# Depthwise convolution, two group norms and a per-row rotation in fp32: beginning, statistics order, transition and second-half loads redone, rotation begun at step 19

## The reference

```python
x = x + conv5x5_depthwise(groupnorm(x), K)          # x: 16 images, 128 channels, 64x64, fp32
x = x + einsum('hvc,bchw->bvhw', R, groupnorm(x))   # R: one 128x128 matrix for each image row h
# groupnorm: 32 groups of 4 channels, mean and variance over (4, 64, 64) of one image, eps 1e-5, no weights
# K: 8 of the 9 weights of a channel, each used once as +w (POS_IDX) and once as -w (NEG_IDX), 9 of 25 places zero
```

## Time and profile before

| | |
|---|---|
| runs of the kernel, without profile | 471.43 us (470.09, 471.43, 472.82) |
| profiled execution, its own time | 474.42 us |
| its span, first to last instruction | 472.5 us |
| last matmul ends / last output store lands | about 442 us / the end of the span |
| TensorE busy | 405.8 us (86%), granted clock 0.963 on the mean |
| VectorE, ScalarE, GpSimd busy | 361.3, 265.8, 232.0 us |
| DMA | 140.63 MB, 298 GB/s over the span |

### The profile page before, as it was taken

How to read it: one execution, slowest core, us unless ns; L and a number is a source line. 1 busy time by engine, 2 the same in 40 slices (tenths; PEclk the granted TensorE clock), 3 DMA queues, 4 the chain that set the end, 5 groups by cost and what they waited for, 6 DMA issues and landing times.

```text
span 472.5 us, 8427 instructions
## 1 busy us (share of the span) xinstructions
PE 405.8 (86%) x3104; PEld 195.0 (41%) x3104; DVE 361.3 (76%) x701; ACT 265.8 (56%) x516; POOL 232.0 (49%) x297
## 2 busy tenths in 40 slices
PE   0498979999999999999999999999995799999400
PEld 0154434555555555554444444434441334444100
DVE  2669999999999999998777877766665678888300
ACT  1144647576766756777666555566633377777000
POOL 3544666676756756776456544454211244545000
PEclk9999999999999999999999999999997999999855
DMA  8805558889998678997598999999979999999995
GB/s 306 365 1 171 188 179 240 281 304 365 372 297 273 207 255 314 388 361 272 185 313 304 324 313 337 312 305 304 307 233 300 308 207 420 379 389 418 427 428 250
DMA packets 33512, 140.63 MB, mean 298 GB/s; under 512 B 3392, under 2 KB 3648, under 8 KB 20800
## 3 DMA queue, kind: packets, MB, share of 16 engines
q1 hardware_dynamic: 16000, 106.24, 63.5%
q10 hardware_dynamic: 17472, 33.85, 20.6%
HBM read 72.96 MB, written 67.12 MB: 296 GB/s over the span
## 4 chain that ended last, share of the span: by engine, by line
PE 71%; DVE 16%; ACT 2%; issue 2%; DMA 2%; ACTq 1%; DVEq 0%
PE ps L612 47%; PE ps L645 23%; DVE stats L514 4%; DVE area L503 2%; DVE area L500 2%; DVE stats L522 2%; DMA rot<-in_taps_first_dram 2%; ACT gn L447 2%; DVE tin L552 1%; DVE dev L542 1%; DVE affine L530 1%; ACT std L459 1%; PE ps L622 1%; DVE affine L532 1%; ACTq L439 1%
## 5 line engine op out<-in xcount | busy, mean ns | idle before, releaser
L612 PE MATMUL ps<-area 64*64 64x496 f32 (+2 forms) x2560 | 287.0, 591 | 7.8 <-issue 4.4
L612 PEld LDWEIGHTS ps<-area 64*64 64x64 f32 x2560 | 137.0, 134 | 107.1 <-issue 97.2
L364 POOL TENSOR_TENSOR area<-mask,area 128x325 f32<-128x325 f32 x128 | 131.9, 1055 | 71.6 <-PE ps L612 53.8
L645 PE MATMUL ps<-gn,rot 128*128 128x512 f32 x256 | 118.6, 608 | 11.6 <-DVE tin L552 7.6
L464 ACT ACTIVATE area<-area,affine 128x256 f32<-128x256 f32 x190 | 96.9, 588 | 30.4 <-DVE affine L532 30.4
L430 ACT ACTIVATE area<-ps 64x512 f32<-64x512 f32 x128 | 75.8, 592 | 42.7 <-PE ps L612 40.1
L522 DVE BATCH_NORM_STATS2 stats<-area 128x6 f32<-128x512 f32 x128 | 80.8, 692 | 0.8
L514 DVE BATCH_NORM_STATS2 stats<-area 128x6 f32<-128x512 f32 x128 | 80.3, 690 | 0.0
L645 PEld LDWEIGHTS ps<-gn,rot 128*128 128x128 f32 x256 | 46.7, 192 | 79.5 <-issue 66.6
L379 POOL TENSOR_SCALAR area<-area,affine 128x256 f32<-128x256 f32 x62 | 46.9, 766 | 65.8 <-DVE affine L532 65.8
L459 ACT ACTIVATE std<-ps,eps 128x16 f32<-128x16 f32 (+1 forms) x36 | 9.8, 273 | 76.7 <-PE ps L622 76.7
(11 more groups left out here) (19 smaller groups left out, 74.9 us busy)
## 6 DMA issues: line engine op xcount, KB each, us to landing
area<-in_x_dram SPq DMA_DIRECT2D x31, 1024.0 KB, 7.3
x_scratch<-area ACTq DMA_DIRECT2D x62, 512.0 KB, 9.6
out_dram<-tin SPq DMA_DIRECT2D x16, 1024.0 KB, 10.2
out_dram<-area SPq DMA_DIRECT2D x16, 1024.0 KB, 25.4
tin<-x_scratch SPq DMA_DIRECT2D x13, 1024.0 KB, 12.5
area<-x_scratch SPq DMA_DIRECT2D x13, 1024.0 KB, 12.3
rot<-in_rota_dram SPq DMA_DIRECT2D x4, 1024.0 KB, 10.8
tin<-x_scratch SPq DMA_DIRECT2D x3, 896.0 KB, 17.5
```

The lines of the kernel that those rows point to most:

```text
L364: last = nc.gpsimd.tensor_tensor(taps[k % TRING][:, c * KW:(c + 1) * KW].rearrange("p d (b r) -> p d b r", r=TAPS), bass.AP(tensor=of_rows ...
L612: last = nc.tensor.matmul(ps[half, bank + c].rearrange("p (j w) -> p j w", j=J)[:, :, outs], taps[k % TRING][rows, (2 * pair + c) * KW + d ...
L645: nc.tensor.matmul(ps[:, rot_bank(m), :], rot[:, n % UNITS * RH + h], gn[n % NRING][:, h], start=True, stop=True).then_inc(rotated, 1)
```

## The change

The beginning: taps come once, unsigned (two DMAs, not four), and the signs are in the mask, which now has one 65-wide band for each of the 5 offsets and is made by GpSimd with 4 more affine_selects, a memset and 10 small tensor_scalars; GpSimd starts on taps only after the first spread is formed; VectorE normalises 3 images of step 0, ScalarE 5; x is measured at most 2 steps ahead in place of 3, the first steps written out. The statistics: VectorE's order in a step changes, own and other adds become two functions, the sums of steps 30 and 31 share the last round (ROUNDS = 35), the averages of mean and spread share bank 7. The rotation: it begins at step 19 and ends there with 13 granules kept (KEPT) before the convolution ends; its four matmuls follow each other at the end of a step, over banks 4, 5, 6, later seven banks. The transition: the last averages stand between rotations of granule 13; norm2 of the last steps of each half goes by small DMAs on SyncE's queue. The loads: six granules of the second half are loaded early from step 28 on, each with the channels that are stored by then (80, 88, 96, 104, 112, 112), the gap up to channel 111 after send_norms of step 29, the last 16 channels after the last x1 store; the other loads and the stores are written out. Host side, the taps arrays are laid out without the plus and minus parts.

```diff
-ROUNDS = STEPS_ALL + LAG
-FILL = 4
+ROUNDS = STEPS_ALL + LAG - 1
+FILL = 2
 POOL_J = 2
-DVE_J = 4
+DVE_J = 3
 RH = 4
 UNITS = H // RH
 GRANULES = 2 * UNITS
-START = 21
+START = 19
 KEPT = STEPS_ALL - START
 DRING = 5
 NRING = 2
+ROT_BANKS = 3
 POOL_IMAGES = 3
 ROT_LOADS = 4
 ROT_STEP = 8
-EARLY_STEPS = PER_HALF - 2
-EARLY = EARLY_STEPS * 2 * GC
-EARLY_COUNT = 6
-NORM2_BATCH = PER_HALF - 2
+NORM2_BATCH = (PER_HALF - 2, PER_HALF - 4)
+EARLY_STEP = 28
+EARLY = tuple(range(EARLY_STEP, EARLY_STEP + 5)) + (EARLY_STEP + 4,)
 def conv_rotate_kernel(nc, x, taps_first, taps_rest, rota, out):
...
-        SWITCH = 2 * (START - 1)
+        SWITCH = 2 * START
         def bank_of(q):
-            return 2 * (q % 3) if q < SWITCH else 2 * ((q + 1) % 2)
+            return 2 * (q % 3) if q < SWITCH else 2 * (q % 2)
...
+        LAST_THREE = KEPT * RH - 1
         def rot_bank(m):
-            return 4 + m % 2 if m < (KEPT + 1) * RH else m % 6
...
+            e = n - UNITS
+            if not 0 <= e < len(EARLY):
+                return 16
+            return 48 if channels_before(EARLY[e] - 2) < LATE else 32
...
+            r, half, first = sum_round(k), k // PER_HALF, k % PER_HALF * 2 * GC
+            queue.wait_ge(affine_ready, r + 1)
+            for n in range(2):
+                queue.dma_start(norm2[first + n * GC:first + (n + 1) * GC, half].rearrange("c k j -> c (k j)"),
+                                affine[n * HALF:n * HALF + GC, r, sum_place(k)].rearrange("p k j -> p (k j)")
+                                ).then_inc(norm2_sent, 16)
         def load_granule(queue, n, channels):
             u = n % UNITS
...
+            sp.dma_start(row_rest.rearrange("p r d -> p (r d)"), taps_rest).then_inc(taps_landed[1], 16)
+            for k in range(4, XRING):
+                load_x(k)
+            for s in range(2, STEPS_ALL + 1):
+                sp.wait_ge(x1_ready, 2 * (s - 1))
...
                     sp.dma_start(rot[:, rows], rota[:, rows]).then_inc(rot_landed, 16)
+                if s == PER_HALF + 1:
...
                     load_granule(sp, 1, slice(0, C))
...
...
+                if s == STEPS_ALL - 1:
+                    store_norms(1)
+                if s == STEPS_ALL:
+                    load_norms(1)
+                    send_norms(sp, STEPS_ALL - 4)
+                n = s - START + 2
+                if n >= 2:
+                    if n >= DRING:
+                        sp.wait_ge(out_stored[n - DRING], 16)
+                    load_granule(sp, n, slice(0, C))
+                for e in range(len(EARLY)):
+                    if EARLY[e] == s:
+                        await_stores(sp, s - 3)
+                        if e == 5:
+                            sp.wait_ge(stats_ready, measured(s - 3 + LAG))
+                        load_granule(sp, UNITS + e, slice(0, channels_before(s - 2)))
+            send_norms(sp, STEPS_ALL - 3)
+            for e in range(len(EARLY)):
+                if channels_before(EARLY[e] - 2) < LATE:
+                    load_granule(sp, UNITS + e, slice(channels_before(EARLY[e] - 2), LATE))
+            send_norms(sp, STEPS_ALL - 2)
+            send_norms(sp, STEPS_ALL - 1)
+            await_stores(sp, STEPS_ALL - 1)
+            for e in range(len(EARLY)):
+                load_granule(sp, UNITS + e, slice(LATE, C))
             store_granule(sp, KEPT - 1)
...
             sp.wait_ge(convolved, 2 * STEPS_ALL)
+            load_granule(sp, 22, slice(0, C))
...
+            for rows in (slice(0, 2), slice(2, RH)):
+                store_rows(sp, GRANULES - 1, rows)
...
+            for n, (d, sign) in enumerate(((0, 1.0), (1, -1.0), (3, -1.0), (4, 1.0))):
+                pool.wait_ge(middle_ready, n + 1)
+                nc.gpsimd.affine_select(out=near_middle[:], in_=near_middle[:], compare_op=ALU.not_equal, fill=sign,
+                                        base=d - PAD, pattern=[[-1, HALF + BAND]], channel_multiplier=1
+                                        ).then_inc(middle_ready, 1)
...
+            for n in range(2):
+                half, window = slice(n * HALF, (n + 1) * HALF), slice(n * HALF, n * HALF + BAND)
+                for d, source, sign in ((0, near, 1.0), (1, near, -1.0), (2, near_middle, 1.0), (3, near, -1.0),
+                                        (4, near, 1.0)):
+                    nc.gpsimd.tensor_scalar(mask[half, d], source[half, window], sign, None, ALU.mult
+                                            ).then_inc(mask_ready, 1)
...
+            pool.wait_ge(spread_ready, 1)
+            spread_taps(0, (0, 1))
+            spread_taps(0, (2, 3))
+            pool.wait_ge(spread_ready, 2)
+            spread_taps(1, (0, 1))
+            normalise(1)
+            spread_taps(1, (2, 3))
+            pool.wait_ge(spread_ready, 3)
+            spread_taps(2, (0, 1))
+            normalise(2)
+            spread_taps(2, (2, 3))
+            spread_taps(3, (0, 1))
+            spread_taps(3, (2, 3))
+            for s in range(FILL, STEPS_ALL - 1):
                 if group(s + 2):
...
+            act.dma_start(row_first.rearrange("p r d -> p (r d)"), taps_first).then_inc(taps_landed[0], 16)
...
+            s = STEPS_ALL - 1
+            evict(s - 1, 1)
+            take_root(s + 1)
+            normalise_rows(KEPT)
+            evict(s, 0)
+            store(act, s - 1)
+            take_root(s + 2)
+            evict(s, 1)
+            store(act, s)
+            normalise_rows(KEPT + 1)
+            take_root(s + 3)
+            for n in range(KEPT + 2, GRANULES):
...
                 c, bank = 2 * pair, bank_of(2 * k + pair)
...
+            def add_other(k, pair):
+                c = 2 * pair + 1
                 dve.wait_ge(y_ready, 2 * (2 * k + pair + 1))
...
+            measure(0, (0, 2, 1, 3))
+            deviate(0)
+            scale(0)
+            dve.wait_ge(affine_ready, 1)
+            for j in range(DVE_J):
+                last = nc.vector.tensor_scalar(normed[0][:, :, j], xin[0][:, j], affine[:, 0, 0, 0, j:j + 1],
+                                               affine[:, 0, 0, 1, j:j + 1], ALU.mult, ALU.add)
+            last.then_inc(normed_dve, 1)
+            measure(1)
+            measure(2, (0,))
+            deviate(1)
+            measure(2, (1, 2, 3))
+            scale(1)
+            add_own(0, 0)
+            measure(3, (0, 1))
+            deviate(2)
+            measure(3, (2, 3))
+            add_other(0, 0)
+            scale(2)
+            add_own(0, 1)
+            add_other(0, 1)
+            measure_sum(0)
+            deviate(3)
+            add_own(1, 0)
+            add_other(1, 0)
+            for s in range(FILL, START):
+                measure(s + 2)
+                scale(s + 1)
+                add_own(s - 1, 1)
+                add_other(s - 1, 1)
+                measure_sum(s - 1)
+                deviate(s + 2)
+                add_own(s, 0)
+                add_other(s, 0)
+            for s in range(START, STEPS_ALL - 1):
+                add_own(s - 1, 1)
+                if group(s + 2):
+                    measure(s + 2)
+                scale(s + 1)
+                add_other(s - 1, 1)
+                measure_sum(s - 1)
+                deviate(s + 2)
+                add_own(s, 0)
+                add_other(s, 0)
+                add_rows(s - START, range(RH))
+            s = STEPS_ALL - 1
+            add_own(s - 1, 1)
+            scale(s + 1)
+            add_other(s - 1, 1)
+            measure_sum(s - 1)
+            deviate(s + 2)
+            add_own(s, 0)
+            add_other(s, 0)
+            add_own(s, 1)
+            scale(s + 2)
+            add_other(s, 1)
+            measure_sum(s)
+            add_rows(KEPT - 1, (0, 1))
+            deviate(s + 3)
+            add_rows(KEPT - 1, (2,))
+            scale(s + 3)
+            add_rows(KEPT - 1, (3,))
+            for n in range(KEPT, GRANULES):
                 add_rows(n, range(RH))
...
+            for half in (low, high):
+                average_mean(0, half)
+            for half in (low, high):
+                average_spread(0, half)
+            for at, d in enumerate(OFFSETS):
+                convolve(0, 0, d)
+                if at in (2, 3):
+                    average_mean(1, low if at == 2 else high)
+                if at == 4:
+                    average_spread(1, low)
+            for at, d in enumerate(OFFSETS):
+                convolve(0, 1, d)
+                if at == 0:
+                    average_spread(1, high)
+                if at in (2, 3):
+                    average_mean(2, low if at == 2 else high)
+            for s in range(1, STEPS_ALL):
                 for at, d in enumerate(OFFSETS):
+                    convolve(s, 0, d)
+                    if at in (0, 1):
+                        average_spread(s + 1, low if at == 0 else high)
                 for at, d in enumerate(OFFSETS):
+                    convolve(s, 1, d)
+                    if at in (0, 1):
```

(42 more changed lines are left out.)

321 lines of the change are left out of this document (121 added, 200 removed).

## The result

The changed kernel takes **453.88 us** (median of 4 runs, 452.9 to 457.95), the kernel before 470.8 in the same comparison: ratio 0.965, interval 0.958 to 0.972. The forecast was 445 with a range of 434 to 460: faster, as forecast, by 3.5% in place of 5.6%. The profiled execution took 454.8 us, its span 453.0 (before 474.42 and 472.5).

What follows compares the result with a forecast made beforehand. TensorE paces the loop until the convolution's end, DMA bandwidth after it: 340 + 26 + 80 = 446 us of span, 448 profiled with 1.9 around it, median 445 us after the 3.0 profile offset; range 434 to 460.

Steps and rivals of the forecast that it cites:

- the walk: First steps: VectorE's written order followed with durations; only step 1's images late for TensorE, by 0.7 us.
- GpSimd starts its first taps at 8.8: Before the first matmul: GpSimd starts at 8.8, a channel pair takes 2.0 us, ready at 10.9.
- to the lower clock: Beginning, before step 6: 3.3 of the 10.7 us lost come from first matmuls at 1.2 GHz until 25.4.
- The rotating step: Loop with rotation: four matmuls together keep one change of matmul kind, so a step falls from 13.27 to 12.54 us.
- 4 to 5 us to land is just enough, at worst one stall of 3 us: Granule 0's norms, sent 4 us into step 18, land before normalising begins at 8 to 9.6.
- The transition: From the last convolution matmul to granule 16's rotation: 26 us, moving 7.3 MB, where it took 32 us.
- B: Rival: loads come no faster, 343 GB/s may be the limit; median 457 us, chance 0.17.
- C: Rival: the beginning gives little, masks late and VectorE as slow as now; 453 us, chance 0.12.
- D: Rival: the transition is short, norms land in 5 us and stores keep 0.41 MB/us; 437 us, chance 0.08.
- F: Rival: four matmuls together still wait for rows, a step stays at 13.3 us; 452 us, chance 0.09.
- E: Rival: SyncE, waiting in the loop for output stores to land, becomes the bound; slower than before, chance 0.04.
- its deciding point: Rival E: an output-store landing of 16.7 us a pass, against the 29 us gained; at 17.5 the time is 483.

Runs made afterwards that it cites:

- Experiment 1: Changed kernel plus twelve spare bn_stats on VectorE ahead of its first measurement: 460.78 us, ratio 0.978 to the kernel before.
- Experiment 2: Changed kernel with the rotation's four matmuls, and add_rows, split again as two and two: 458.1 us, ratio 0.973 to the kernel before.
- experiment 3: Changed kernel with only banks 4 and 5 for the rotations inside the loop, bank 6 left empty: 455.05 us, ratio 0.967 to the kernel before.
- experiment 5: Changed kernel with send_norms of step 15 issued ahead of SyncE's wait for x1_ready: 448.18 us, ratio 0.953 to the kernel before.
- experiment 8: Changed kernel with output stores of granules 12 to 14 issued ahead of SyncE's wait for the last x1 store: 450.49 us, ratio 0.955.
- its control: The changed kernel once more, unedited, run beside the kernels of later experiments: 453.32 us, ratio 0.964 to the kernel before.
- experiments 1 to 5: Adds number 4: changed kernel with rotation from step 21, some loads and stores moved behind the loop: 452.51 us, ratio 0.961.
- experiments 1, 2, 3, 5 and 7: Adds number 7: changed kernel without the output stores of granules 18 to 25 (8.4 MB not written): 438.02 us, ratio 0.928.

## Why the prediction was right, and where it was off

**The beginning: right.** Forecast 12.9 us earlier at step 6, measured 12.1. The last convolution pairs of the plain loop come at their 4.33 us with one wait of 0.58 us for GpSimd, in step 1, where the walk had 0.7. (By the letter a wait of TensorE in the first five steps was to be a sign of being wrong, though the walk itself had this one.) Spread and square are small again before the first matmul, and the mask multiplications took 0.4 us each (0.72 for two), the upper bound, where I took 0.25. GpSimd was still ready in time: at 9.0. The first matmul was off by 1.2 us: scale and bias were ready at 10.4, not 10.0, and I had costed ScalarE's five images (ready at 13.0), not VectorE's three beside GpSimd (13.7). The step "GpSimd starts its first taps at 8.8" was wrong too, since the taps land at 10.4, but its first pair was ready at about 12.5 and nothing waited for it. The 3.3 us "to the lower clock" rest on the lengths of the first matmuls: in the kernel before, eight records took 1.99 us from 18.84 on, where eight take about 0.85 later; the granted clock of the profile reads 1.00 there, so the clock is inferred and not shown. Experiment 1 shows that a delay of the first matmul goes through to the end one for one.

**The rotating step: right.** 12.50 for 12.54. Experiment 2 gives the single term, 0.40 for 0.43, experiment 3 the third bank, 0.20 where I had a wait of zero "if VectorE is there".

**The convolution's end: 4.8 us late.** The step that failed is "4 to 5 us to land is just enough, at worst one stall of 3 us". The norms took 6.5 us to land, TensorE waited 2.3 us, and then ran at a granted clock of 0.64 and 0.82 (1.2 GHz for part of the time), which cost 1.9 more. That was priced as a mishap outside the sum, and was 4.3 us of the 4.8; experiment 5 takes it away. 0.8 came from the beginning, and the steps gave 0.5 back. The wait was found by following who is queued behind the waiting instruction: not the rotation, which had time, but GpSimd's taps for the convolution.

**The transition: 28.4 us for 26, at 215 GB/s for 280.** The bandwidth is the term that was mis-sized: the DMA engines run out of requests at about 362, the last x1 store lands at 367, and the order of SyncE's queue lets nothing else be asked for until then. The first 15 us ran at 292, no worse than forecast. The thirteen microseconds at 129 GB/s are two different losses:

```profile
362.00:367.30 5.30, 0.00 (x0) 0.00 (x0) 0.18 (x1) 0.00 (x0) 0.00 (x0) 0.65 0.42 107
367.30:373.40 6.10, 0.04 (x1) 0.05 (x1) 0.00 (x0) 2.66 (x6) 2.58 (x5) 0.50 0.92 121
```

In the first the DMA share is 0.42: requests are missing, and experiment 8 fills this part. Against 396 GB/s it is (396 - 107) x 5.3 = 1.5 MB, some 3.9 us by estimate. In the second, with the six late loads of 16 channels under way, the share is 0.92 and the rate is 121 GB/s all the same; by the same estimate that is 1.7 MB or 4.2 us, and experiment 8 only moves it (share 1.00 at 110 GB/s from 373.4 to 376 us in its kernel). Why these loads are slow was not tried. Bytes by stretch: 28.4 x 215 = 6.1 MB, 79.6 x 396 = 31.5, together 37.6 of the 38.4 forecast.

**What sets the end: right.** 79.6 us for 80. From granule 16's start to the end of the span it was 78.3 to 79.9 us in the changed kernel, its control and experiments 1 to 5, whatever the steps before looked like, 82 us where 0.66 MB more were left, and 70.5 where three output stores had gone ahead (experiment 8). The rivals: B (the loads come no faster) fell by what it said would follow, since 139.8 - 37.6 = 102.2 MB had been moved by the convolution's end, where the forecast had 101.4, and nothing arrived late. Its sign in the loop didn't decide: 319 GB/s lies between B's "under 310" and the forecast's 330, and 319 / 0.93 is the same 343 GB/s that B named, so by this rate alone B's figure isn't excluded. Against it stand 409 GB/s over 6.7 us in the loop of experiment 5, ahead of the first output store, and 396 behind the loop. The bound of about 358 GB/s a core that the Trainium skill states (DMA: Bandwidth & Descriptors, "Where 436 GB/s comes from") is not what this kernel meets there, with 396 GB/s over 79.6 us. C, D and F didn't come about. E didn't either (its deciding point took 29 us gained from a profiled time less the forecast median; like for like it is 26.4, and the point 16.5 us, which changes nothing): the output stores of the loop landed in 5.2 to 10.7 us, under a step, as the view of L234 up to 345 us says:

```profile
DMA to landing us min/median/max: 5.2/9.4/10.7
```

**The sum.** 446 + 4.8 + 2.4 (transition) - 0.4 is 452.8, the span is 453.0. The plain median lay 0.9 under the profiled execution, where I had taken 3.0 off; that is 2 of the 9 us between forecast and median.

**What stays open.** Why the norms' 0.2 KB DMAs took 5.9 to 8.3 us in the chains of waits of these kernels wasn't tried beyond moving them. The parts of experiment 5's gain, wait and clock, are read from the traces; no run has one without the other. Early loads from step 28 on were not tried against the earlier placement.

## What to carry to other kernels

Where the end is a draining DMA queue, count bytes that may be asked for, not TensorE's schedule: a stretch in which the issuing engine waits for one landing while finished output rows lie ready cost 3 to 4 us here in the timed runs, and was repaired by moving three stores ahead of the wait, although that made the next matmul later. A change that moves work earlier (here the start at step 19) can lose all its worth if its first operand lands late and the engine that waits for it also feeds the main loop; send such small operands ahead of the queue's own waits.

## What was not expected of the hardware

A wait of 2.3 to 3.7 us of TensorE, in a loop where it had been busy throughout, was followed by a granted clock of 0.64 over the next 3.1 us and 0.82 over the 3.2 after (1.2 GHz for part of each), in the control by 0.56 over the next 3.4 us; the convolution's end came 4 to 5 us earlier without it. And the last x1 store, 2 x 512 KB issued on ScalarE's queue, took 15.8 to 19.7 us to land in the changed kernel, its control and experiments 1, 2, 3, 5 and 7, with SyncE's loads issued beside it, and 14.0 and 15.7 in the two kernels with 0.66 MB of them left out: the queue it is issued on didn't shield it.
